# Score and gate/up products of a six-layer kernel: f32 matmuls replaced by three rounded ones

## The reference

```
tensor = qr.kr + qi.ki          spinor = qr.ki - qi.kr
wedge  = sqrt(max(|q|^2 |k|^2 - tensor^2 - spinor^2, 0) + 1e-6)
hodge  = sqrt(|q|^2 + 1e-6) * sqrt(|k|^2 + 1e-6)
scores = (geo0*wedge + geo1*tensor + geo2*spinor + geo3*hodge) / 4 / temperature
out    = softmax(scores) @ V, then an output projection
```

## Time and profile before

| | us |
|---|---|
| median of 3 runs (2866.30 to 2882.51) | 2876.18 |
| the profiled execution | 2878.03 |
| its span, first to last instruction | 2876.3 |
| PE busy | 2463.9 |
| DVE busy | 1651.9 |
| ACT busy | 1351.8 |

### The profile page before, as it was taken

The page is one execution under the profiler, slowest core; times in us unless marked ns, Lnnn a source line. Parts: engine busy times, 40 slices in busy tenths (PEclk is TensorE's granted clock), DMA queues, the critical chain, the costliest instruction groups (busy, mean ns, idle before and its releaser), DMA issues. The chain is left out here.

```text
span 2876.3 us, 31392 instructions
## 1 busy us (share of the span) xinstructions
PE 2463.9 (86%) x11368; PEld 1457.5 (51%) x11368; DVE 1651.9 (57%) x3418; ACT 1351.8 (47%) x1968; POOL 327.6 (11%) x299
## 2 busy tenths in 40 slices
PE   6998898866888888879999799995688888887998
PEld 3666666652333333335566465654455555554565
DVE  5666656624666666645543789896655666532222
ACT  3333333311555555543221756562577777861211
POOL 1010010000000000000266100000211111100000
PEclk8899889966999999989899899997899999998999
DMA  2000000005233333204045321111201000002000
GB/s 76 8 15 15 15 15 15 8 8 162 52 67 67 67 67 60 52 25 143 28 68 72 76 67 46 66 54 61 75 15 37 30 30 23 23 8 66 22 15 22
DMA packets 104945, 132.41 MB, mean 46 GB/s; under 512 B 21748, under 2 KB 87556, under 8 KB 104792
## 3 DMA queue, kind: packets, MB, share of 16 engines
q1 hardware_dynamic: 90440, 115.58, 15.0%
q0 software_dynamic: 11904, 14.69, 3.2%
q10 hardware_dynamic: 2448, 0.14, 0.1%
HBM read 73.69 MB, written 31.20 MB: 36 GB/s over the span
## 5 line engine op out<-in xcount | busy, mean ns | idle before, releaser
L987 DVE TENSOR_REDUCE xattn_tops<-region 128x2 f32<-128x1024 f32 x256 | 306.3, 1220 | 123.5 <-PE region L771 123.4
L924 ACT ACTIVATE xattn_probs<-region 128x1024 f32<-128x1024 f32 x256 | 256.2, 1022 | 123.6 <-PE region L760 122.3
L2165 PE MATMUL region<-psi_fT 128*128 128x512 f32 x512 | 230.9, 597 | 10.2 <-ACT psi_fT L2289 7.0
L156 PE MATMUL region<-gla_xT,weights_even 128*128 128x512 f32 (+1 forms) x416 | 201.6, 639 | 20.3 <-ACT gla_xT L248 20.3
L760 PE MATMUL region<-xattn_qs,xattn_ks 49*128 49x512 f32 x512 | 125.1, 490 | 62.3 <-DVE xattn_tops L987 31.4
L156 PE MATMUL region<-mamba_xT,weights_odd 128*128 128x512 f32 x320 | 155.7, 633 | 3.1 <-DVE mamba_xh L1988 3.1
L2165 PEld LDWEIGHTS region<-psi_fT 128*128 128x128 f32 x512 | 93.6, 190 | 126.3 <-issue 115.0
L156 PEld LDWEIGHTS region<-gla_xT,weights_even 128*128 128x128 f32 (+1 forms) x416 | 77.8, 194 | 133.6 <-issue 107.4
L789 PE MATMUL region<-xattn_probs,xattn_va 128*32 128x512 f32 x1024 | 141.0, 618 | 1.2 <-ACT xattn_o_T L951 1.2
L771 PE MATMUL region<-xattn_ks,xattn_qs 48*128 48x512 f32 x512 | 124.0, 482 | 13.6 <-DMA xattn_ks<-xattn_khi 9.2
L165 PE MATMUL region<-weights_even,gla_work 128*128 128x256 f32 x512 | 119.7, 394 | 17.6 <-DVE gla_work L631 11.0
(11 more groups left out here) (506 smaller groups left out, 5086.3 us busy)
## 6 DMA issues: line engine op xcount, KB each, us to landing
weights_even<-mamba_cs SPq DMA_DIRECT2D x32, 512.0 KB, 4.7
xattn_qs<-xattn_qhi SPq DMA_DIRECT2D x128, 64.0 KB, 2.3
xattn_ks<-xattn_khi SPq DMA_DIRECT2D x128, 64.0 KB, 2.3
moe_sums<-moe_picked SPq DMA_DIRECT2D x9, 512.0 KB, 7.8
gla_x<-in_x SPq DMA_DIRECT2D x8, 512.0 KB, 3.8
x_after_gla<-gla_res SPq DMA_DIRECT2D x8, 512.0 KB, 2.9
xattn_x<-x_after_gla SPq DMA_DIRECT2D x8, 512.0 KB, 4.1
xattn_ctxT<-in_ctxT SPq DMA_DIRECT2D x8, 512.0 KB, 4.3
```

Source lines behind the costliest of these rows:

```text
L156: last = st.nc.tensor.matmul(o[0:m, i, :], w[:, c, col + i * P:col + i * P + m], rhs[:, c, :], start=c == 0, stop=c == kc - 1)
L924: A_(probs[:, p % 3, a, :, :], st.region(f"k{v}")[:], ACT.Exp).then_inc(st.emptying(f"k{v}"), 1)
L987: V.tensor_reduce(tops[:, n % 2, t, a::2], st.region(f"q{u}")[:], AX, ALU.max).then_inc(st.emptying(f"q{u}"), 1)
L2165: last = mm(o[:, a, :], fT[:, h, 0, t * P:t * P + P], fT[:, h, 1 + a, :], start=True, stop=True)
```

## The change

In psi the 64 quadratic numbers of a group are split into a rounded part (F32R) and the rest. A score's first region half becomes the sum of two rounded products over 128 rows: (query high, query low) x (key high, key high) and (query high, query low) x (key low, 0 or 0, key low by head), the second half one rounded product over the 17 linear numbers, laid out as high, high, low against high, low, high. DVE makes the parts in two new "split" steps, and "fT" has seven transposing steps instead of four. turns and angle lie in the second product buffer, scores and ctxv have one buffer each. In ffn gate and up are sums of three rounded products each. The relu step's code is the same. The core of the diff:

```diff
+        turns, angle = (prods[:, 1, :, :, :].rearrange("p g d n -> p (g d n)")[:, 512 * i:512 * i + 512].rearrange(
+            "p (a n) -> p a n", a=2) for i in range(2))
+        tQ, tK, tL = st.sb("tQ", [GQ, 2, 64], F32R), st.sb("tK", [GQ, 2, 64], F32R), st.sb("tL", [GQ, 64], F32R)
+        tS = st.sb("tS", [G2, 64], F32R)
+        fA, fL = st.sb("fA", [GH, 2, T], F32R), st.sb("fL", [GH, T], F32R)
+        fQ, fK = st.sb("fQ", [2, T], F32R), st.sb("fK", [GH, T], F32R)
-        scores = [st.sb("scores", [GQ, T])[:], spare]
+        scores = K["rooms"][0][:, 1024:1024 + GQ * T].rearrange("p (i n) -> p i n", i=GQ)
+        TURNS = (("wide", 0), ("rest", 0), ("narrow", 0), ("wide", 1), ("wide", 2), ("rest", 1), ("wide", 3))
+        NEEDS = {0: (0, 1, 2), 1: (3,), 2: (4, 5), 3: (6,)}
...
                 yield "sums", b - 1, 0
+                yield "fT", b, 4
                 yield "score", b, 3
...
                 yield "turn", b - 1, 7
+                yield "fT", b, 5
                 yield "score", b, 5
                 yield "features", b + 1, 3
                 yield "score", b, 6
+                yield "fT", b, 6
...
                 yield "scaled", b - 1, 0
+                yield "split", b + 1, 0
                 yield "features", b + 1, 5
...
                 yield "score", b, 11
+                yield "split", b + 1, 1
...
-                        for a in range(2):
-                            last = mm(o[:, a, :], fT[:, h, 0, t * P:t * P + P], fT[:, h, 1 + a, :],
-                                      start=True, stop=True)
-                        last.then_inc(st.filling(f"s{b}_{i}"), 1)
+                        q = fA[:, h, 0, t * P:t * P + P]
+                        mm(o[:, 0, :], q, fA[:, h, 1, :], start=True, stop=False)
+                        mm(o[:, 0, :], q, fL[:, h, :], start=False, stop=True)
+                        mm(o[:, 1, :], fQ[:, h // 2, t * P:t * P + P], fK[:, h, :], start=True, stop=True).then_inc(
+                            st.filling(f"s{b}_{i}"), 1)
...
                 def load_ctxv(b):
-                    if b >= 2:
-                        sp.wait_ge(*st.full(f"pv{b - 2}_{DC - 1}"))
+                    if b:
+                        sp.wait_ge(*st.full(f"pv{b - 1}_{DC - 1}"))
...
-                        A_(fT[0:FW, i, 0, :], o[0:FW, 0, :], ACT.Copy)
-                        A_(fT[0:64, i, 1, :], o[0:64, 1, :], ACT.Copy)
-                        A_(fT[64:FW, i, 2, :], o[64:FW, 1, :], ACT.Copy).then_inc(
+                        if kind == "wide":
+                            last = A_(fA[:, n, :, :], o[:], ACT.Copy)
+                        elif kind == "rest":
+                            A_(fL[0:64, 2 * n, :], o[0:64, 0, :], ACT.Copy)
+                            A_(fL[64:P, 2 * n + 1, :], o[64:P, 0, :], ACT.Copy)
+                            last = A_(fQ[:, n, :], o[:, 1, :], ACT.Copy)
+                        else:
+                            A_(fK[0:64, 0::2, :], o[0:64, :, :], ACT.Copy)
+                            last = A_(fK[64:P, 1::2, :], o[64:P, :, :], ACT.Copy)
...
+                def split_of(b, i):
+                    if i == 0:
+                        dve.wait_ge(st.sem("paired"), b + 1)
+                        if b:
+                            dve.wait_ge(*st.full(f"fT{b - 1}_{len(TURNS) - 1}"))
+                        V.tensor_copy(q_high, q_wide)
+                        step(V.tensor_copy(tK[:], feat[:, kg, 0:64].unsqueeze(2).to_broadcast([P, GQ, 2, 64])))
+                        TT(q_low, q_wide, q_high.bitcast(F32), ALU.subtract)
+                        TT(tL[:], feat[:, kg, 0:64], tK[:, :, 0, :].bitcast(F32), ALU.subtract)
+                    else:
+                        narrow, high = feat[:, :, 64:FW], tS[:, :, 0:17]
+                        step(V.tensor_copy(high, narrow))
+                        V.tensor_copy(tS[:, qg, 17:34], high[:, qg, :].bitcast(F32))
+                        V.tensor_copy(tS[:, kg, 34:51], high[:, kg, :].bitcast(F32))
+                        TT(tS[:, qg, 34:51], narrow[:, qg, :], high[:, qg, :].bitcast(F32), ALU.subtract)
+                        TT(tS[:, kg, 17:34], narrow[:, kg, :], high[:, kg, :].bitcast(F32), ALU.subtract).then_inc(
                             st.sem("featured"), 1)
...
-                            if j == 0 and b >= 2:
-                                dve.wait_ge(*st.full(f"pT{b - 2}_{GH - 1}_1"))
+                            if j % NT == 0 and b:
+                                dve.wait_ge(*st.full(f"pT{b - 1}_{j // NT}_1"))
...
                             for c in range(DC):
-                                last = mm(o[:, a, :], wide[n][:, c, e * P:e * P + P], xT[:, b % 2, c, :],
-                                          start=c == 0, stop=c == DC - 1)
+                                for k, (w, v) in enumerate(((whi, xhi), (wlo, xhi), (whi, xlo))):
+                                    last = mm(o[:, a, :], w[n][:, c, e * P:e * P + P], v[:, b % 2, c, :],
+                                              start=c == 0 and k == 0, stop=c == DC - 1 and k == 2)
...
-                A_(wide["w_up"][:], wide["w_up"][:], ACT.Copy, scale=1.0 / 127.0).then_inc(st.sem("wide_w_up"), 1)
+                A_(w_down[:], w_down[:], ACT.Copy, scale=1.0 / 127.0).then_inc(st.sem("w_down"), 1)
...
-                        A_(xT[:, b % 2, :, :], st.region(f"xT{b}")[:], ACT.Copy).then_inc(st.emptying(f"xT{b}"), 1)
+                        A_(xhi[:, b % 2, :, :], st.region(f"xT{b}")[:], ACT.Copy).then_inc(st.sem("xhi"), 1)
...
+                def low(b):
+                    dve.wait_ge(st.sem("xhi"), b + 1)
+                    V.tensor_tensor(xlo[:, b % 2, :, :], st.region(f"xT{b}")[:], xhi[:, b % 2, :, :].bitcast(F32),
+                                    ALU.subtract).then_inc(st.emptying(f"xT{b}"), 1)
...
+                for n in ("w_gate", "w_up"):
+                    V.tensor_scalar(whi[n][:], weights[n].bitcast(I32), 1.0 / 127.0, None, ALU.mult).then_inc(
+                        st.sem(f"split_{n}"), 1)
+                    dve.wait_ge(st.sem(f"split_{n}"), 1)
+                    V.scalar_tensor_tensor(wlo[n][:], weights[n].bitcast(I32), 1.0 / 127.0, whi[n][:].bitcast(F32),
+                                           ALU.mult, ALU.subtract).then_inc(st.sem(f"split_{n}"), 1)
+                    if n == "w_gate":
+                        low(0)
```

More of the change, by code:

```diff
@@ L2040, in psi_layer @@
         xs = [st.sb(f"x{i}", [NT, D]) for i in range(XS)]
-        ctxvs = [st.sb(f"ctxv{i}", [NT, D]) for i in range(2)]
+        ctxv = st.sb("ctxv", [NT, D])
         ctxT, featT = st.sb("ctxT", [DC, T]), st.sb("featT", [DC, T])
@@ L2239, in _ @@
                 load_x(2)
-                load_ctxv(1)
                 load_x(3)
@@ L2246, in _ @@
                         load_ctxT(b + 1)
-                    elif what == "score" and i == 11 and 2 <= b + 1 < B:
-                        load_ctxv(b + 1)
+                    elif what == "score" and i == 11 and b:
+                        load_ctxv(b)
                     elif what == "norm":
@@ L2302, in _ @@
                         for k in range(NT * i, NT * i + NT):
-                            last = A_(scores[b % 2][:, k, :], scores[b % 2][:, k, :], ACT.Exp, scale=-1.0,
+                            last = A_(scores[:, k, :], scores[:, k, :], ACT.Exp, scale=-1.0,
                                       bias=low[:, b % 2, k:k + 1], accum_out=sums[:, b % 2, k:k + 1])
@@ L2445, in _ @@
                         features_of(b, i)
+                    elif what == "split":
+                        split_of(b, i)
                     elif what == "angles":
@@ L2506, in ffn_layer @@
         ident = K["ident"]
-        x, xT, h = st.sb("x", [B, NT, D]), st.sb("xT", [2, DC, T]), st.sb("h", [2, HF, T])
+        x, h = st.sb("x", [B, NT, D]), st.sb("h", [2, HF, T])
+        xhi, xlo = (st.sb(n, [2, DC, T], F32R) for n in ("xhi", "xlo"))
         silu, shift = st.sb("silu", [2, T]), st.sb("shift", [2, NT])
         norms = [Norm(st, s) for s in range(2)]
-        wide = {n: st.sb(n, list(weights[n].shape[1:])) for n in ("w_gate", "w_up", "w_down")}
+        whi, wlo = ({n: st.sb(f"{n}_{part}", [DC, HID], F32R) for n in ("w_gate", "w_up")} for part in ("hi", "lo"))
+        w_down = st.sb("w_down", list(weights["w_down"].shape[1:]))
         def order():
@@ L2552, in _ @@
                         if b == 0:
-                            pe.wait_ge(st.sem("wide_w_down"), 1)
+                            pe.wait_ge(st.sem("w_down"), 1)
                         for e in range(HF - 3, HF):
@@ L2558, in _ @@
                             for c in range(HF):
-                                last = mm(o[:, t * D:t * D + D], h[:, b % 2, c, t * P:t * P + P], wide["w_down"][:, c, :],
+                                last = mm(o[:, t * D:t * D + D], h[:, b % 2, c, t * P:t * P + P], w_down[:, c, :],
                                           start=c == 0, stop=c == HF - 1)
@@ L2602, in _ @@
```

(15 more changed lines are left out.)

47 lines of the change are left out of this document (30 added, 17 removed).

## The result

The changed kernel takes 2831.32 us (median of 4 runs, 2822.73 to 2834.78) where the kernel before takes 2879.35 us: a ratio of 0.9846, with a 95% interval of 0.9811 to 0.9881. Predicted were 2821 us, with 2785 to 2850 as the range. The profiled execution took 2834.78 us (span 2833.1), 43.2 less than the profiled one before.

A forecast was written before the change was run, and what follows sets the result against it. PE was taken to bound ffn throughout, and no single engine psi. From the profiled 2878.0 us, 38.7 for ffn and 17 for psi were taken off: 2822, against the median 2820.5, said as 2821; range 2785 to 2850.

The forecast's parts named there:

- The price of a rounded product: One rounded product of 512 columns over 128 rows on PE: 0.216 us taken, 0.23 as the other end.
- ffn's start: DVE's subtraction comes between ACT's copy and ffn's first product: 1.2 us lost, leaving 38.7 us gained in ffn.
- psi, steady: psi's iteration from sine to sine falls from 68.2 to 63.5 us, or 66.1 with PE at half clock, which was taken.
- A: psi iteration's first stretch, to the end of DVE's score 8: from 26.0 to 27.1 us, plus 1.9 for half clock.
- B: psi iteration's second stretch, to the last square root: from 22.0 to 16.4 us, with DVE becoming the bound.
- C: psi iteration's third stretch, exponentials to the sine, set by ACT: stays 20.0 us, plus 0.7 for half clock.
- the last two iterations: End of psi: next to last gains 1 us together with the first; the last gains 5, from 51.5 us.
- At nothing: Priced at no cost: single score and context buffers, angles inside the product buffer, and the first fill of zeros.
- rival 1: psi follows PE fully, clock holds, splits hide in DVE's idle time: psi gains 74 us, 2765 us in all; chance 0.20.
- under 60: Sign of rival 1: psi's period from sine to sine under 60 us.
- over 68: Sign that psi pays its gain back (psi +8 instead of -17, 2847 us; chance 0.18): psi's period over 68 us.
- over 3.4 us: Sign that a rounded product takes two passes, 0.43 us (2951 us in all; chance 0.04): an ffn hidden tile over 3.4.

The follow-up runs named there:

- psi_nosplit: Changed kernel with psi's high/low split on VectorE done for the first batch only (output not the reference's): 2815.8 us, ratio 0.9775 to the kernel before.
- psi_warm: Changed kernel with score 2's three products done four times over in TensorE's rest at an iteration's start: 2818.8 us, ratio 0.9812 to the kernel before.
- psi_warm_dve: Changed kernel with the repeats of psi_warm_all and three copy groups of transposed features moved from ScalarE to VectorE: 2837.3 us, ratio 0.9881 to the kernel before.
- psi_warm_all: Changed kernel with score 2's products done five times and some transposes two or three times, filling TensorE's rests: 2834.3 us, ratio 0.9848 to the kernel before.

## Why the prediction was right or wrong

**The price of a rounded product: the term that was mis-sized.** I took 0.216 from the f32 record and put the row of the only rounded products in the trace, the pair 0.23 apart, at the other end. The pair was right: 0.2333, 17 ns more for each of the 12 products of 47 tiles, 9.8 of the 11 us that ffn came out short. My reason for 0.216 (weights change every 0.216 us without loss) was sound but answered another question: the loads are hidden even at a pitch of 0.12, and it is the columns that stream slower. It is nearly all of what the whole time missed, 2831 us for 2821. The Trainium skill (TensorE: Matmul & The Clock Gate, section "Wait — 56ns, not 53.3ns?") gives 215.7 ns from start to start for 512 columns once warm and 426.7 cold; this trace agrees cold (0.43) and does not for a rounded product at full clock (0.2333).

**ffn's start.** Predicted 1.2 us lost, measured 1.2 to 1.3. With tiles of 2.80 instead of 3.43 (13.73 / 4; 0.63 x 47 = 29.7), less 1.3 and less 0.7, ffn should gain 27.7; it gained 27.8. The 0.7 is the half clock at the start, which I put at nothing: it held for all twelve products of the first tile, not only for the six that I named, and the first four tiles took 2.62 us more than later ones instead of 1.91.

**psi, steady.** A was predicted at 27.1 us and 29.0 with the clock, B at 16.4, C at 20.0 and 20.7: 66.1. Measured are 27.9, 17.1 and 19.8: 64.8. DVE's splits took 4.2 and 1.7 us where 4.3 and 1.7 were priced, and DVE waited 0.8 us in B. ACT's copies I added up wrongly: my own terms give 9.7 us where I wrote 9.2, and they took 9.5. The clock fell where I said it would in A (0.53 over 6 us) and not in C. In the terms of the Trainium skill's section "A second HAM failure mode: psum-queue depth-cycling" (TensorE: Matmul & The Clock Gate), PE does fall between its clocks once an iteration here. The five intervals from the third on gained 15.0 us together where I had 11; the first two 1.9.

**psi, the last two iterations.** Here I was wrong, and the error hid the one before. I had 1 us for the first and the next to last iteration together and 5 for the last; behind the last sine, where the last two lie, 0.4 was lost (146.4 for 146.0). The last iteration took 48.99 us instead of 51.51, ACT's 43.62 plus 5.4 of waits, and the tail behind it lost 1.7 of those 2.5: its first value products took 5.26 us at a granted clock of 0.68, where the same sixteen took 3.65 before. The next to last lost 1.3 us where I had it gain; without its split it is 5.3 shorter (psi_nosplit), and with PE's rest filled the stretch behind the last sine is 3.5 shorter (psi_warm). That psi as a whole came out at 16.5 us for 17 is luck: 4 us too little for the five intervals from the third on, 4.5 too much for the ends. The first value products of the tail, before and after:

```profile
2570.70 3.65 PE L2188 MATMUL region<-psi_pT,psi_ctxv 128*64 128x512 f32 x16 [2.44 <-DVE psi_pT L2453]
```
```profile
2553.70 5.26 PE L2209 MATMUL region<-psi_pT,psi_ctxv 128*64 128x512 f32 x16 [1.56 <-DVE psi_pT L2505]
```

**At nothing.** The waits for the single score and context buffers do not appear in psi's waits after the change, and the angles in the product buffer neither.

**The rivals.** The period is neither under 60 nor over 68, a tile is not over 3.4 us. What speaks for rival 1 (PE's time simply comes off) is the edges; against it, psi_nosplit, with less work in B, and psi_warm, ahead in A, kept the steady 64.8. Since the clock fell at another place in each, and what had been won was lost there, the clock may be what holds it; shown is the loss, at the place where the window says half clock, not that the period would fall without it. The two iterations of psi_warm_dve at full clock took 64.87 us as well, so with other work in the queues the period is as long without any half clock. What sets the steady period stays open.

## What to carry to other kernels

Price an operation from the row that is like it in type and passes, even with other shapes, before a row of another type that fits the shape; of two ends, the like one was the right one here. In a queue of several engines, taking 1 us off one stretch is worth nothing until the next wait has been named: psi_nosplit took 5.4 us of VectorE's work out of a steady iteration and left its period at 64.8. And before tuning a split into high and low parts, ask whether the operand needs one: whole numbers of 8 bits do not, and that was worth more than all of psi.

## What was not expected of the hardware

- A rounded 32-bit product streams at 0.443 ns a column at full clock (0.2333 us for 512, 0.1198 for 256), where the passes of an f32 record take 0.42; at half clock it is 0.43 us for 512.
- 128x128 weights can change every 0.12 us, though each load is recorded with 0.19: they overlap the products and one another.
- The half clock moved. Filled at one place of an iteration it came at another, some 17 us (psi_warm) or 8 us (psi_warm_all) later, and the steady period was 64.7 to 65.2 us in four kernels with different work in it. In two iterations of psi_warm_dve it did not come at all, and the period was 64.87.
